# Expert tiles of a mixture-of-experts layer: 32 of 256 rows and 7 of 128 instead of 39 of 256

## The reference

```python
for e in range(E):                     # 8 experts, each token goes to its top 2
    h = jax.nn.gelu(xf @ w1[e] + b1[e], approximate=False)   # 256 -> 1024
    out = out + comb[:, e:e + 1] * (h @ w2[e] + b2[e])       # 1024 -> 256
x = x + tanh(g_ffn) * out
```

## Time and profile before

| | us |
|---|---|
| median of 3 runs | 992.07 (989.59 to 993.5) |
| profiled execution, its span | 992.7 |
| first stage and the change of stage, to the first matmul of tile 0's input | 549.0 |
| 39 tiles on TensorE, one tile in full swing | 10.92 |
| TensorE busy / VectorE / ScalarE / GpSimd | 832.3 / 517.9 / 376.7 / 438.1 |
| mean granted TensorE clock | 0.914 of full speed |

### The profile page before, as it was taken

How to read it: one execution, slowest core, us unless ns; L and a number is a source line. 1 busy time by engine, 2 the same in 40 slices (tenths; PEclk the granted TensorE clock), 3 DMA queues, 4 the chain that set the end, 5 groups by cost and what they waited for, 6 DMA issues and landing times. The chain is left out here.

```text
span 992.7 us, 20863 instructions
## 1 busy us (share of the span) xinstructions
PE 832.3 (84%) x6508; PEld 579.8 (58%) x6509; DVE 517.9 (52%) x1534; ACT 376.7 (38%) x770; POOL 438.1 (44%) x475
## 2 busy tenths in 40 slices
PE   3675899899898989887610899999999999999994
PEld 1243345344343534433310699899989989988984
DVE  3475567766766677762330345444544454454451
ACT  1312263636363544666320333333333433333330
POOL 4766463666566545436541033333433343333334
PEclk9867899989997989898755799999999999999998
DMA  4653424433445261244224122221332233223210
GB/s 160 147 108 107 75 66 90 129 82 108 97 128 98 64 136 49 82 134 138 77 74 165 56 44 46 48 45 33 56 48 41 43 58 48 43 47 49 44 14 1
DMA packets 65691, 76.40 MB, mean 77 GB/s; under 512 B 7392, under 2 KB 59360, under 8 KB 65504
## 3 DMA queue, kind: packets, MB, share of 16 engines
q1 hardware_dynamic: 51328, 58.74, 22.7%
q0 software_dynamic: 14304, 16.93, 9.6%
HBM read 47.68 MB, written 29.53 MB: 78 GB/s over the span
## 5 line engine op out<-in xcount | busy, mean ns | idle before, releaser
L2389 PE MATMUL ps_h<-x_hi,w_split 128*128 128x256 bf16 x1248 | 212.7, 274 | 0.0
L2403 PE MATMUL ps_y<-w_split,hidden 128*128 x1248 | 206.4, 273 | 0.0
L698 ACT ACTIVATE prob<-ps_a 128x512 f32<-128x512 f32 x192 | 113.0, 603 | 181.5 <-PE ps_a L1127 108.2
L2389 PE MATMUL ps_h<-x_lo,w_split 128*128 128x256 bf16 x624 | 171.0, 274 | 0.0
L2403 PE MATMUL ps_y<-w_split,h_lo 128*128 x624 | 170.1, 273 | 0.0
L2299 ACT ACTIVATE hidden<-ps_h,bias 128x256 f32<-128x256 f32 x312 | 131.1, 471 | 88.6 <-PE ps_h L2389 88.6
L849 DVE TENSOR_REDUCE row_max<-ps_d 128x2 f32<-128x384 f32 x237 | 127.9, 551 | 60.8 <-PE ps_d L1107 59.2
L2273 POOL DMA_INDIRECT out<-y,token_at x78 | 131.0, 1680 | 43.8 <-POOL token_at L2271 30.3
L2389 PEld LDWEIGHTS ps_h<-x_hi,w_split 128*128 x1248 | 122.8, 98 | 14.5
L2403 PEld LDWEIGHTS ps_y<-w_split,hidden 128*128 128x128 bf16 x1248 | 122.1, 98 | 14.1
L2269 POOL TENSOR_TENSOR token_f<-tails,ones_f 128x2 f32<-128x2 f32 x39 | 7.8, 200 | 267.5 <-DVE y L2345 266.3
(11 more groups left out here) (206 smaller groups left out, 1070.8 us busy)
## 6 DMA issues: line engine op xcount, KB each, us to landing
w_stage<-w SPq DMA_DIRECT2D x32, 512.0 KB, 4.1
xg<-queue SPq DMA_DIRECT2D x39, 260.0 KB, 2.8
w_split<-q_split SPq DMA_DIRECT2D x24, 256.0 KB, 7.9
x_in<-x SPq DMA_DIRECT2D x8, 512.0 KB, 3.8
ctx_sb<-ctx_t SPq DMA_DIRECT2D x8, 512.0 KB, 3.6
x<-x SPq DMA_DIRECT2D x8, 512.0 KB, 3.8
q_split<-q_hl SPq DMA_DIRECT2D x16, 256.0 KB, 3.5
out<-x SPq DMA_DIRECT2D x8, 512.0 KB, 5.0
```

The costliest lines, as they stand in the source:

```text
L698: a.activation(prob[n % 2][:, j, :], ps_a[i % 2][:], ACT.Exp, scale=SCALE).then_inc(exp_ready, 1)
L2389: last = t_.matmul(ps_h[n][:, c, :], k.w1_split[:, bass.ds(e, 1), part, kt, f].rearrange("p a f -> p (a f)"), xs[s][:, kt, :], start=(q == ...
L2403: last = t_.matmul(ps_y[s][:, t, :], hs[s][:, f, token], k.w2_split[:, bass.ds(e, 1), part, f, :].rearrange("p a d -> p (a d)"), start=(q ...
```

## The change

The table now has 32 tiles of 256 rows and 7 of 128. Each queue is counted in halves of 128 rows (ceil of its rows by 128): pairs of halves are served first, by the big tiles, then the odd half of each queue that has one. If there are fewer than 32 pairs, the remaining big tiles take single halves; the small ones take the rest, and empty ones read the dummy queue. 8192 rows make at most 71 halves, that is 2 x 32 + 7. There are 39 tiles as before.

In a small tile (i from 32 on) every engine works on one block of 128 rows: 128 moving columns in the first layer, one block and 24 matmuls in the second, 2 transposes, half the columns on ScalarE and VectorE, one indirect DMA on GpSimd.

TensorE's order changes from body 33 on: a quarter of the first layer of tile i (12 matmuls), then a quarter of the second layer of tile i-1 (6), four times. Both expert numbers are loaded at the start of the body; the waits of the second layer (begin_layer2) come after the first quarter of the first layer. Body 32 still computes the whole second layer of tile 31, a big one. The loop covers tiles 2 to 29, and tiles 30 to 38 are written out.

The table pass on VectorE works with 16 parts (8 of pairs, 8 of singles) by 39 tiles instead of 8 by 39, and has some short operations more; GpSimd fills a few more constants at the start. The two callers give tile_tables a second scratch tile.

```diff
-N_TILES = (2 * B * L + E * (TILE - 1)) // TILE
+N_BIG, N_SMALL = 2 * B * L // TILE, E - 1
+N_TILES = N_BIG + N_SMALL
+HALVES = (B * L + TILE) // P
...
+def tile_tables(v, chain, k, scratch, more_scratch):
+
+    S = 2 * E
+    table = N_TILES * S
+    mine, past = (part[:, 0:table].rearrange("p (i e) -> p i e", e=S) for part in (scratch, more_scratch))
+    full = scratch[:, 0:E * HALVES].rearrange("p (e n) -> p e n", e=E)
+    first_row, valid, left = (more_scratch[:, table + c * N_TILES:table + (c + 1) * N_TILES] for c in range(3))
+    every = lambda a: a[:, None, :].to_broadcast([P, N_TILES, S])
+    each = lambda a: a[:, :, None].to_broadcast([P, N_TILES, S])
+    pairs, single = k.part_len[:, 0:E], k.part_len[:, E:S]
...
+    chain.step(v.tensor_reduce(pairs, full[:, :, 1::2], AX.X, ALU.add))
+    chain.then(v.tensor_reduce(single, full, AX.X, ALU.add))
...
+    chain.then(v.scalar_tensor_tensor(out=k.entry[:], in0=k.tile_cap[:], scalar=k.n_pairs[:, 0:1], in1=k.tile_no[:], op0=ALU.min, op1=ALU.add))
+    chain.step(v.tensor_tensor(mine, each(k.entry), every(k.part_len), ALU.is_ge))
+    chain.then(v.tensor_tensor(past, each(k.entry), every(k.part_end), ALU.is_ge))
...
+            g.iota(k.tile_cap[:, 0:N_BIG], pattern=[[1, N_BIG]], base=0, channel_multiplier=0, allow_small_or_imprecise_dtypes=True)
...
+            g.memset(k.tile_cap[:, N_BIG:N_TILES], float(N_BIG))
+            g.iota(k.half_row[:], pattern=[[P, HALVES]], base=0, channel_multiplier=0, allow_small_or_imprecise_dtypes=True)
...
-            with engine.Fori(1, (N_TILES - 3) // 2) as j:
+            with engine.Fori(1, (N_BIG - 2) // 2) as j:
                 body(2 * j, j, 0, True, True)
                 body(2 * j + 1, j, 1, True, True)
-            for i in range(2 * ((N_TILES - 3) // 2), N_TILES):
+            for i in range(2 * ((N_BIG - 2) // 2), N_TILES):
                 body(i, i // 2, i % 2, i + 1 < N_TILES, i + 2 < N_TILES)
...
+        def blocks(i):
+
+            return 1 if isinstance(i, int) and i >= N_BIG else 2
+
+        def rows_of(i):
+            return blocks(i) * P
+
+        def adds(i):
+
+            return 32 * i if not isinstance(i, int) or i <= N_BIG else 32 * N_BIG + 16 * (i - N_BIG)
...
-                sp.dma_start(xg[s][:], k.queue[bass.ds(row, TILE)].rearrange("(s p) c -> p s c", p=P)).then_inc(row_loaded[s], 16)
+                sp.dma_start(xg[s][:, 0:blocks(i)], k.queue[bass.ds(row, rows_of(i))].rearrange("(s p) c -> p s c", p=P)
+                             ).then_inc(row_loaded[s], 16)
...
-                    pool.wait_ge(added, 32 * i)
+                    pool.wait_ge(added, adds(i))
                 pool.wait_ge(y_weighted, i + 1)
-                chain.then(g.tensor_tensor(token_f[:], tails[:, bass.ds(i, 1), :, 3].rearrange("p a s -> p (a s)"),
-                                           k.ones_f[:, 0:2], ALU.mult))
-                chain.then(g.tensor_copy(token_at[:], token_f[:]))
-                for t in range(2):
+                n = blocks(i)
+                chain.then(g.tensor_tensor(token_f[:, 0:n], tails[:, bass.ds(i, 1), 0:n, 3].rearrange("p a s -> p (a s)"),
+                                           k.ones_f[:, 0:n], ALU.mult))
+                chain.then(g.tensor_copy(token_at[:, 0:n], token_f[:, 0:n]))
+                for t in range(n):
...
-                        last = a.activation(hidden[s][:, f, :], ps_h[n][:, c, :], ACT.Gelu, bias=bias[s][:, f:f + 1])
+                        last = a.activation(hidden[s][:, f, 0:rows_of(i)], ps_h[n][:, c, 0:rows_of(i)], ACT.Gelu, bias=bias[s][:, f:f + 1])
...
-                v.tensor_tensor(x_lo[s][:], ps_x[:], x_hi[s][:], ALU.subtract).then_inc(x_lo_ready, 1)
+                v.tensor_tensor(x_lo[s][:, :, 0:rows], ps_x[:, :, 0:rows], x_hi[s][:, :, 0:rows], ALU.subtract).then_inc(x_lo_ready, 1)
...
-                v.tensor_tensor(y[s][:], ps_y[s][:], b2_own, ALU.add).then_inc(y_biased, 1)
+                b2_own = b2_all[:, bass.ds(e, 1), :].to_broadcast([P, blocks(i), D])
+                v.tensor_tensor(y[s][:, 0:blocks(i)], ps_y[s][:, 0:blocks(i)], b2_own, ALU.add).then_inc(y_biased, 1)
                 dve.wait_ge(y_biased, i + 1)
-                for t in range(2):
+                for t in range(blocks(i)):
...
-                    v.tensor_tensor(h_lo[s][:, both, :], hidden[s][:, both, :], h_hi[s][:, both, :], ALU.subtract
+                    both, rows = slice(2 * n, 2 * n + 2), slice(0, rows_of(i))
+                    v.tensor_tensor(h_lo[s][:, both, rows], hidden[s][:, both, rows], h_hi[s][:, both, rows], ALU.subtract
...
-                    for t in range(2):
+                    for t in range(blocks(i)):
...
-            def layer1(i, s):
-                e = load_expert(pe, i)
-                pe.wait_ge(x_lo_ready, i + 1)
-                for n in range(PAIRS):
-                    if not first(i):
-                        pe.wait_ge(gelu_done, PAIRS * (i - 1) + n + 1)
-                    for c in range(2):
-                        f = slice((2 * n + c) * P, (2 * n + c + 1) * P)
-                        terms = [(kt, part, xs) for kt in range(KT) for part, xs in ((0, x_hi), (0, x_lo), (1, x_hi))]
-                        for q, (kt, part, xs) in enumerate(terms):
-                            last = t_.matmul(ps_h[n][:, c, :],
-                                             k.w1_split[:, bass.ds(e, 1), part, kt, f].rearrange("p a f -> p (a f)"),
-                                             xs[s][:, kt, :], start=(q == 0), stop=(q == len(terms) - 1))
-                    last.then_inc(h_ready, 1)
-
-            def layer2(i, s):
-                e = load_expert(pe, i)
+            def layer1(i, s, e, n):
+                if not first(i):
+                    pe.wait_ge(gelu_done, PAIRS * (i - 1) + n + 1)
+                for c in range(2):
+                    f = slice((2 * n + c) * P, (2 * n + c + 1) * P)
+                    terms = [(kt, part, xs) for kt in range(KT) for part, xs in ((0, x_hi), (0, x_lo), (1, x_hi))]
+                    for q, (kt, part, xs) in enumerate(terms):
+                        last = t_.matmul(ps_h[n][:, c, 0:rows_of(i)],
+                                         k.w1_split[:, bass.ds(e, 1), part, kt, f].rearrange("p a f -> p (a f)"),
+                                         xs[s][:, kt, 0:rows_of(i)], start=(q == 0), stop=(q == len(terms) - 1))
+                last.then_inc(h_ready, 1)
+
+            def layer2(i, s, e, t, fs):
+                token = slice(t * P, (t + 1) * P)
+                for f in fs:
+                    for q, (hs, part) in enumerate(((h_hi, 0), (h_hi, 1), (h_lo, 0))):
+                        last = t_.matmul(ps_y[s][:, t, :], hs[s][:, f, token],
+                                         k.w2_split[:, bass.ds(e, 1), part, f, :].rearrange("p a d -> p (a d)"),
+                                         start=(f == 0 and q == 0), stop=(f == FC - 1 and q == 2))
+                if t == blocks(i) - 1 and f == FC - 1:
+                    last.then_inc(y_summed, 1)
+
+            def begin_layer2(i):
                 pe.wait_ge(h_lo_ready, PAIRS * (i + 1))
                 if not first(i, 2):
                     pe.wait_ge(y_weighted, i - 1)
-                terms = [(f, hs, part) for f in range(FC) for hs, part in ((h_hi, 0), (h_hi, 1), (h_lo, 0))]
-                for t in range(2):
-                    token = slice(t * P, (t + 1) * P)
-                    for q, (f, hs, part) in enumerate(terms):
-                        last = t_.matmul(ps_y[s][:, t, :], hs[s][:, f, token],
-                                         k.w2_split[:, bass.ds(e, 1), part, f, :].rearrange("p a d -> p (a d)"),
-                                         start=(q == 0), stop=(q == len(terms) - 1))
-                last.then_inc(y_summed, 1)
+
+            def whole_layer2(i, s):
+                e = load_expert(pe, i)
+                begin_layer2(i)
+                for t in range(blocks(i)):
+                    layer2(i, s, e, t, range(FC))
 
             def body(i, half, s, more, two_more):
                 if more:
                     turn(i + 1, half + s, 1 - s)
-                layer1(i, s)
-                if not first(i):
-                    layer2(i - 1, 1 - s)
+                e = load_expert(pe, i)
+                if isinstance(i, int) and i > N_BIG:
+                    past = load_expert(pe, i - 1)
+                pe.wait_ge(x_lo_ready, i + 1)
+                for n in range(PAIRS):
+                    layer1(i, s, e, n)
+                    if isinstance(i, int) and i > N_BIG:
+                        if n == 0:
+                            begin_layer2(i - 1)
+                        layer2(i - 1, 1 - s, past, 0, range(2 * n, 2 * n + 2))
+                if not first(i) and not (isinstance(i, int) and i > N_BIG):
+                    whole_layer2(i - 1, 1 - s)
 
             turn(0, 0, 0)
             over_tiles(pe, body)
-            layer2(N_TILES - 1, (N_TILES - 1) % 2)
```

(32 more changed lines are left out.)

30 lines of the change are left out of this document (20 added, 10 removed).

## The result

The changed kernel takes 968.53 us (median of 4 runs, 967.88 to 969.38); the kernel before 992.79 (4 runs, 989.59 to 993.56). The ratio is 0.977, 95% interval 0.975 to 0.979. The forecast was 966.7 us.

A forecast was written before the change was run, and what follows sets the result against it. The expert stage was taken as bound by TensorE's array, small tiles by its sequencer: 992.7 - 21.1 (bodies) - 4.3 (tail) = 967.3, less 0.6 gives 966.7 us; 962 to 972 by its terms, wider range 952 to 977.

The forecast's parts named there:

- The sequencer sets 8.0 us a small tile: TensorE's sequencer in small tiles: 48 weight addresses of 0.13 us plus loads and waits take 8.0 us, the array 5.5.
- Rival A: Small tiles: TensorE's array decides, not its sequencer, 5.5 us a tile; whole kernel 952.3 us; chance 0.13.
- Body 32 9.1 us, body 33 6.2, four of 8.0, body 38 7.8, last tile ends 21.1 us earlier: TensorE's bodies 32 to 38: from 898.1 us to 953.2, where body 38 ended at 974.34 before.
- 128 columns, 55 ns: First layer of small tiles: a 128-column matmul takes 55 ns, half of 109 for 256, its weight load hidden.
- Gap of about 1.3 us at each tile's start: Sign in bodies 34 to 37: TensorE's busy rows show this idle while the expert numbers load.
- Waits of the alternating order covered: Second layer of tile i-1 waiting for its low halves: 1.5 us needed, 3.1 us issued between, covered by 1.6.
- Clock at 1.00: Sign in the small tiles: TensorE's granted clock stays at 1.00 (2.4 GHz).
- B: Rival: idle of about 1.3 us per small tile drops TensorE's clock to 1.2 GHz; 10.7 us a tile, 986.5; chance 0.06.
- Tail saves 4.3: From body 38's end to the end of the span: 14.1 us instead of 18.4, with half-size last tiles.
- Table pass hidden by 10 us of cover: VectorE's longer table pass adds 4.2 us, ending at 526.7; next stage begins at 537.2, so it costs nothing.
- The profiled execution's own time is the span, and 0.6 comes off: Before: span 992.7, median of three runs 992.07; so 0.6 us was taken from the 967.3 sum.
- D: Rival: TensorE waits for code blocks of nine written-out tiles, 3.75 us each, 33.7 in all; 1000.4 us; chance 0.04.

## Why the prediction held, step by step

- *The sequencer sets 8.0 us a small tile*: right, and shown three ways: without addresses 5.7, with loads moved away 6.6, with four more such tiles + 9.9 us. Rival A falls.
- *Body 32 9.1 us, body 33 6.2, four of 8.0, body 38 7.8, last tile ends 21.1 us earlier*: they took 9.4, 6.31, 32.0 together and 7.75, so 55.4 us against the 55.1 of the sum, and the lead of the sequencer was used up in one tile, as worked out. (The sum ends body 33 at 913.4, where its own terms, 905.1 + 8.0, give 913.1; the 0.3 has no reason there.) That the end nevertheless came 21.5 us earlier is luck: bodies 0 to 31, of which 0.2 was to go, took 348.3 us from the first turn against 349.3 before, and four more executions with large tiles throughout stand at 348.6 to 349.1.
- *128 columns, 55 ns*: 56.
- *Gap of about 1.3 us at each tile's start*: 0.98 to 1.05; the remainder shows as a first quarter of 1.10 instead of 0.67.
- *Waits of the alternating order covered*: right; no releaser from another engine stands in bodies 33 to 38. (In body 32 the page names VectorE's low halves ahead of the second layer, 0.7 us, but that layer needs those of tile 31, done a body earlier; its first address is computed at 902.1, after the load, and the array begins at 902.25.) But I did not ask what the alternation is worth at all. It is worth nothing measurable.
- *Clock at 1.00*: right, and by less room than the chance of 0.06 for B said: with one load more, 0.7 us of idle more in a tile, it fell.
- *Tail saves 4.3*: 4.9. From body 38's end to the last scatter 6.95 us, as worked out (7.0); from that scatter to the end of the span 6.5, where I had carried over the 7.2 of the earlier trace rows.
- *Table pass hidden by 10 us of cover*: wrong, 2.7 us by its own experiment. I looked at what comes after VectorE in its own chain and found slack; what ran beside it, GpSimd's scatters, had none. They show 1.1 of the 2.7.
- *The profiled execution's own time is the span, and 0.6 comes off*: wrong. The profiled execution of the changed kernel took 969.38 us with a span of 967.2. The span was forecast as 967.3; that it came out so close is luck, by differences that cancel (1.0 us more won in the expert stage, 0.8 of it in bodies that the change leaves alone, and 1.0 lost ahead of it); the four runs stand 2.1 to 2.3 us above their spans, where I had put - 0.6, and the median came out 1.8 above the forecast.
- *Faster 0.92, all but D and half of B*: these terms add up to 0.93.

## What to carry to other kernels

Before halving a tile, count the sequencer's instructions in it, not only the array's columns: an address computed from a register cost 0.13 us here for 128 columns as for 256, and a load of an index some 0.7 us wherever the sequencer had no slack. Read such indices once, under work that leaves the sequencer slack, and ask of a new order of work what it hides before writing it. An operation off the chain is free only if what runs beside it on the chain does not slow down.

## What the hardware showed beyond expectation

- In the expert stage TensorE's clock fell from 1.00 (2.4 GHz) to 0.50 (1.2 GHz) behind gaps of 1.65 to 1.76 us, all in the kernel with one load more, and held behind those of 0.87 to 1.11 us there and elsewhere; a slowed array lets its sequencer get ahead and so shortens the next gap, which makes slow and fast tiles alternate (9.58, 7.94, 9.31, 7.96).
- Three of GpSimd's eight indirect scatters took 1.24 to 1.47 us instead of 0.96 beside VectorE operations of 624 elements, in every kernel with the new table of 39 tiles; one beside the first two of those operations took 0.99, and with the old table, beside operations of 312, none but the first (1.11 with either table) took longer than 0.99.
- The time of a run stands 1.7 to 3.1 us above its span, and by how much changes with the kernel: 1.8 in the kernel before run again, 2.1 to 2.3 in the changed one. No experiment was made on this.
